# Gated cross-attention with a mixture of experts: eight normalised tiles made by ScalarE instead of VectorE

## What is computed

```
x: (2, 1024, 256)   ctx: (2, 64, 256)   16 heads of 64   8 experts, 2 used per batch
xn  = layernorm(x)
q   = xn @ Wq ; k = ctx @ Wk / 8 ; v = ctx @ Wv          (per head)
x1  = x + tanh(g_xattn) * (softmax(q k^T) v @ Wo + bo)
y   = layernorm(x1)
pick 2 experts per batch from mean_over_tokens(y) @ gate_w ; shares from a softmax over the two
out = x1 + tanh(g_ffn) * sum_e share_e * (gelu(y @ w1[e] + b1[e]) @ w2[e] + b2[e])
```

## Time and profile before

| | |
|---|---|
| median of three runs | 321.4 us (321.29 to 321.45) |
| span of the profiled execution | 319.0 us (its total is not given; the runs lie 2.4 us above the span) |
| VectorE busy | 236.4 us, 563 instructions |
| ScalarE busy | 164.6 us, 577 instructions |
| GpSimd busy | 84.4 us, 158 instructions |
| chain that ended last | PE 73%, POOL 10%, issue 7%, DVE 6%, ACT 2% |
| mean granted TensorE clock | 0.999 of full speed |

### The profile page before, as it was taken

The page is one execution under the profiler, slowest core; times in us unless marked ns, Lnnn a source line. Parts: engine busy times, 40 slices in busy tenths (PEclk is TensorE's granted clock), DMA queues, the critical chain, the costliest instruction groups (busy, mean ns, idle before and its releaser), DMA issues.

```text
span 319.0 us, 5709 instructions
## 1 busy us (share of the span) xinstructions
PE 313.3 (98%) x1861; PEld 269.8 (85%) x1861; DVE 236.4 (74%) x563; ACT 164.6 (52%) x577; POOL 84.4 (26%) x158
## 2 busy tenths in 40 slices
PE   8999999999999999999999999999999999999996
PEld 7978997879988999888788888888887899888896
DVE  1989999889989998999998475566766554442643
ACT  2658575686766768766466254443542442321320
POOL 1416547585476655526500000000000000000000
PEclk9999999999999999999999999999999999999999
DMA  7997200300000009500016340000020000000012
GB/s 275 385 322 10 33 3 1 134 1 3 0 0 3 0 4 346 179 3 0 2 8 256 95 171 0 0 0 0 33 100 2 2 0 0 2 0 0 4 64 67
DMA packets 21918, 19.99 MB, mean 63 GB/s; under 512 B 11708, under 2 KB 17540, under 8 KB 21508
## 3 DMA queue, kind: packets, MB, share of 16 engines
q1 hardware_dynamic: 21616, 19.14, 20.0%
q10 hardware_dynamic: 276, 0.52, 0.4%
HBM read 17.56 MB, written 2.11 MB: 62 GB/s over the span
## 4 chain that ended last, share of the span: by engine, by line
PE 73%; POOL 10%; issue 7%; DVE 6%; ACT 2%; DMA 1%; POOLq 0%; DVEq 0%
PE ps L1154 22%; PE ps L1155 22%; PE ps L1156 22%; POOL sx L504 4%; PE ps L1174 2%; POOL xs L524 2%; PE ps L1239 2%; POOL xs L522 2%; ACT sx L636 1%; DMA wk_sb<-in_L_xattn_Wk_dram 1%; DVE mx L904 1%; PE ps L1196 1%; DVE pT_lo L863 1%; PE ps L1327 1%; DVE sm L874 1%
## 5 line engine op out<-in xcount | busy, mean ns | idle before, releaser
L723 ACT ACTIVATE gel<-ps,b1sel 128x512 f32<-128x512 f32 x64 | 43.9, 690 | 95.5 <-PE ps L1156 95.5
L1113 DVE CAST h_hi<-gel 128x512 fp32r<-128x512 f32 x64 | 28.4, 444 | 58.8 <-ACT gel L723 58.5
L636 ACT ACTIVATE sx<-ps,mx 128x64 f32<-128x64 f32 x128 | 38.3, 325 | 26.4 <-DVE mx L904 26.3
L1154 PE MATMUL ps<-yT_hi,w_hi 128*128 128x512 f32 (+1 forms) x128 | 50.5, 395 | 0.0
L1155 PE MATMUL ps<-yT_lo,w_hi 128*128 128x512 f32 (+1 forms) x128 | 50.0, 390 | 0.0
L1156 PE MATMUL ps<-yT_hi,w_lo 128*128 128x512 f32 (+1 forms) x128 | 49.9, 390 | 0.0
L1115 DVE TENSOR_TENSOR h_lo<-gel,h_hi 128x512 fp32r<-128x512 f32 x64 | 44.9, 701 | 2.2
L504 POOL TENSOR_TENSOR sx<-sx,rs 128x512 f32<-128x512 f32 x32 | 33.5, 1066 | 41.5 <-DVE rs L879 40.8
L1154 PE MATMUL ps<-h_hi,w_hi 128*128 128x512 f32 x96 | 38.4, 400 | 0.0
L1156 PE MATMUL ps<-h_hi,w_lo 128*128 128x512 f32 x96 | 37.5, 390 | 0.0
L1155 PE MATMUL ps<-h_lo,w_hi 128*128 128x512 f32 x96 | 37.4, 390 | 0.0
(11 more groups left out here) (149 smaller groups left out, 670.0 us busy)
## 6 DMA issues: line engine op xcount, KB each, us to landing
stage_w<-in_L_ffn_w_dram SPq DMA_DIRECT2D x7, 1024.0 KB, 7.4
out_dram<-xt SPq DMA_DIRECT2D x6, 256.0 KB, 2.3
wqT<-in_L_xattn_Wq_dram SPq DMA_DIRECT2D x2, 512.0 KB, 6.9
wv_sb<-in_L_xattn_Wv_dram SPq DMA_DIRECT2D x2, 512.0 KB, 8.5
wo_sb<-in_L_xattn_Wo_dram SPq DMA_DIRECT2D x1, 1024.0 KB, 13.4
xt<-in_x_dram SPq DMA_DIRECT2D x1, 1024.0 KB, 10.4
xs<-in_xT_dram SPq DMA_DIRECT2D x1, 1024.0 KB, 11.2
spread<-x_stat SPq DMA_DIRECT2D x1, 1024.0 KB, 4.6
```

The costliest lines, as they stand in the source:

```text
L636: last = nc.scalar.activation(sx[:, par, c0:c0 + M], ps[:, 2 * par + 1, c0 - BANK:c0 - BANK + M], ACT.Exp, bias=mx[:, par, h:h + 1], accum ...
L723: nc.scalar.activation(gel[:, f % 4, :], ps[:, h_bank, :], ACT.Gelu, bias=b1sel[:, b, slot, f:f + 1]).then_inc(gelu_done, 1)
L1113: nc.vector.tensor_copy(h_hi[:, f % 4, :], gel[:, f % 4, :]).then_inc(hhi_ready, 1)
L1154: mm(acc, hi_w, hi_x, start=start, stop=False)
```

## The change

The VectorE function `y_tile` and its calls are gone. ScalarE has a `y_tile` in its place, called in its step s after `y_high` and before the late `vw` groups and `heads(s)`. It computes scale * x + bias, with scale = rstd2 and bias = shift2 = -mean2 * rstd2. The new small tensor `shift2` is made by GpSimd with two instructions behind the Newton steps, for the parts of the first batch, ahead of the post of `y_rstd`. The waits on `y_rstd` and on the buffer (`yT_done`) are the same and are now ScalarE's.

```
+    shift2 = place("shift2", [P, TB])
...
             def y_rstds(i):
 
                 newton(*Y_PARTS[i], rstd2, ve_y, len(X_PARTS) + i + 1)
+                if Y_PARTS[i][0] < TB:
+                    tiles = slice(*Y_PARTS[i])
+                    link(nc.gpsimd.tensor_tensor(shift2[:, tiles], mean2[:, tiles], rstd2[:, tiles], ALU.mult))
+                    link(nc.gpsimd.tensor_scalar(shift2[:, tiles], shift2[:, tiles], -1.0, None, ALU.mult))
                 pool.sem_inc(y_rstd, 1)
...
+            def y_tile(t):
+
+                act.wait_ge(y_rstd, t // 4 + 1)
+                wait_pos(act, yT_done, t - 1)
+                nc.scalar.activation(yb[:, t % 2, :], xt[:, t, :], ACT.Identity, scale=rstd2[:, t:t + 1],
+                                     bias=shift2[:, t:t + 1]).then_inc(y_ready, 1)
...
                 for y in (Y_WITH_X.get(s), Y_AFTER.get(s)):
                     if y is not None:
                         y_high(y, 7, D, y + 1)
+                for y in (Y_WITH_X.get(s + 1), Y_AFTER.get(s + 1)):
+                    if y is not None:
+                        y_tile(y)
                 if s == NT - 1:
                     w1_high(0)
...
                 if s == 14:
                     y_guess((s - 6) // 4)
-                for y in (Y_WITH_X.get(s + 1), Y_AFTER.get(s + 1)):
-                    if y is not None:
-                        y_tile(y)
...
-            def y_tile(t):
-
-                dve.wait_ge(y_rstd, t // 4 + 1)
-                wait_pos(dve, yT_done, t - 1)
-                nc.vector.tensor_scalar(yb[:, t % 2, :], xt[:, t, :], mean2[:, t:t + 1], rstd2[:, t:t + 1],
-                                        ALU.subtract, ALU.mult).then_inc(y_ready, 1)
```

## The result

The changed kernel takes 324.07 us (median, 323.86 to 324.32), the kernel before 321.35 us (321.04 to 321.45). The ratio is 1.0078, 95% interval 1.0056 to 1.0100: 2.5 us slower (1.8 to 3.2). The prediction was 324.2. The span of the profiled execution went from 319.0 to 321.9 us. Busy time moved as intended, VectorE from 236.4 down to 231.0 us and ScalarE from 164.6 up to 168.0.

What follows compares the result with a forecast made beforehand. TensorE, 98% busy, was taken as the bound, with the ScalarE-VectorE loop of 6.95 us close behind. 2.30 - 0.65 - 0.48 + 0.59 + 1.00 = 2.76 us on the median of 321.4 gave 324.2 us, range 322.3 to 325.3.

Steps and rivals of the forecast that it cites:

- The three places: Where lateness arises: ScalarE's hold in step 7, GpSimd's added time at tile 10, two y tiles ahead of heads 12.
- GpSimd's p = 0.59: Time of GpSimd's two added instructions behind the Newton steps in steps 7 and 11: 0.59 us, bounds 0.40 and 0.8.
- ScalarE's x = 0.50: ScalarE's time for one 128x256 y tile with per-partition scale and bias: 0.50 us, bounds 0.31 and 1.0.
- The hold of step 7, 2.30: In step 7 ScalarE's y tile 0 waits for the first y_rstd, making heads of tile 7 2.30 us late.
- the slack of step 10, 0.48: In step 10 VectorE's pT_lo started 0.48 us later than it could, so that much lateness is absorbed.
- slack of 0.65: VectorE's pT_lo of tile 6 started 0.65 us later than it could, so 2.30 us of lateness leaves 1.65.
- Step 11 and 12: Tile 10's product 1.76 us late; two y tiles ahead of heads of tile 12 add 1.00, making 2.76.
- (a): Rival, 12%: buffers absorb step 7's hold; only 0.59 at 98.86 and part of step 12 reach TensorE: 0.6 to 1.3, 322.4 us.
- (b): Rival, 12%: none of the 0.65 + 0.48 slack absorbs anything and a y tile takes 0.66: 4.4, 325.8 us.
- (c): Rival, 6%: y tiles arrive early, TensorE's waits of 0.31 + 0.26 go, decided in step 7: 320.8 us.
- (d): Rival, 6%: gains and losses cancel over the kernel, within 0.6 us, 321.4.
- 0.08 + 2p + 3x: The whole forecast slowdown in GpSimd's added time p and ScalarE's time per y tile x: 2.76 us.

Runs made afterwards that it cites:

- pool_only: The kernel before with only GpSimd's two small instructions per Newton part added, result unread, VectorE still making all y tiles; 321.70 us, ratio 1.0011.
- one_pool_op: The changed kernel with one GpSimd instruction instead of two, VectorE's statistics halving the mean sum with -0.5 for the first batch; 323.26 us, ratio 1.0054.
- tiles67_dve: The changed kernel with y tiles 6 and 7 made by VectorE again, ScalarE making tiles 0 to 5; 323.31 us, ratio 1.0064.
- best_c: The changed kernel with one GpSimd instruction, three y buffers, and y tiles 6 and 7 ahead of the wait for tile 5's transpose; 322.54 us, ratio 1.0044.
- best_split: best_c with GpSimd's Newton steps begun one step earlier, 8 of 13 instructions in its idle wait; 320.69 us, ratio 0.9977.
- before_split: The kernel before, y tiles on VectorE, with only GpSimd's Newton steps begun one step earlier; 320.93 us, ratio 0.9991.
- after_split: The changed kernel with GpSimd's Newton steps begun one step earlier, 8 of 13 instructions in its idle wait; 321.31 us, ratio 1.0000.
- act_only: The changed kernel without GpSimd's two instructions, ScalarE taking mean2 as bias, so y is shifted wrongly; 322.30 us, ratio 1.0035.

## Why the prediction was right

The three places and the way they add up were right. The sum of 2.76 us met 2.7 in the trace (2.62 at TensorE's last instruction) and 2.5 (1.8 to 3.2) timed. That it fits to a tenth is partly luck, since two of its terms were each wrong by about 0.25 us, in opposite directions. The 2.4 us that the prediction puts on top of the span compare one execution's span with the median of others; by their own spans nearly all executions here lie 2.0 us above it. The forecast is the median of before plus the sum, so this does not enter it. Step by step:

*What is removed.* Right that the eight VectorE instructions are worth almost nothing where they stood: they lay under heads, and VectorE's wait for pT_hi grew from 1.4 to 8.3 us. TensorE's two waits for y tiles went, as said, but a new wait of 0.34 us for tile 6's product, at 71.45, stands in the place of the first, so nothing was won by it: y tile 0 is 0.11 late.

*GpSimd's p = 0.59.* GpSimd's rows of step 7, with the last Newton instruction (477), the second new one (485) and the product behind it (509):

```profile
68.38 0.20 POOL L477 TENSOR_TENSOR rstd<-nu_p,rstd 128x4 f32<-128x4 f32 x1
...
68.94 0.23 POOL L485 TENSOR_SCALAR shift<-shift 128x4 f32<-128x4 f32 x1
69.35 2.04 POOL L509 TENSOR_TENSOR sx<-sx,rs 128x512 f32<-128x512 f32 x2 [0.18 <-POOL shift L485]
```

From the end of the Newton steps at 68.58 to the end of the new instructions at 69.17 it is 0.59. pool_only and one_pool_op showed that it counts at tile 10 and, with tiles on ScalarE, a second time through the hold. One reading was inexact without consequence: the prediction adds 2.10 to 96.76, and the row has 2.04, so the product ended at 98.80, 0.06 before TensorE started.

*ScalarE's x = 0.50.* Measured 0.51 in step 7 (69.25 to 69.76) and 0.49 in step 12 (106.52 to 107.50 for two). The latency was 0.587 to 0.687 us by the y tile's row in the trace, median 0.60, where I had 0.66. The Trainium skill, "ScalarE: Activation LUTs", section What ACT_TABLE_LOAD costs, gives 186 ns plus 0.833 ns per element and about 93 ns for each per-partition operand, with 93 ns of overlap. The estimate from these figures for 256 elements and two such operands is 0.585 us, and 0.49 us to the next instruction. The trace agrees: 0.587 us at the least, 0.49 and 0.51 to the next instruction. The rule of the same page that I weighed in the prediction, VectorE for adds and multiplies, is given there for bf16 and was no guide to the price in float32.

*The hold of step 7, 2.30, and the slack of step 10, 0.48.* These two terms were wrong and cancelled by luck. Heads of tile 7 were 2.07 late, not 2.30. I had counted 1.35 us from the vw groups to heads, but in the kernel before the row maxima ended only at 68.52, and heads started at 68.55 right behind them. In the changed kernel the maxima are long there, and it is 1.14 (69.76 to 70.90). pT_lo of tile 6 was 1.42 late, so the slack of 0.65 held, and steps 8 and 9 added nothing, as forecast (heads 1.43 and 1.41 late). Then step 10 took up 0.23, not 0.48: pT_lo of tile 8 was 1.19 late. The rows of VectorE and GpSimd in the changed kernel show where the rest went:

```profile
85.83 0.43 DVE L967 BATCH_NORM_STATS2 stats<-xt 128x6 f32<-128x256 f32 x1
86.29 0.70 DVE L777 TENSOR_TENSOR dm<-stats 128x4 f32<-128x4 f32 x1
86.91 0.15 DVE L778 TENSOR_TENSOR mean<-stats 128x4 f32<-128x4 f32 x1
```

```profile
86.08 0.89 POOL L529 TENSOR_TENSOR xs<-xs,spread 128x256 f32<-128x256 f32 x1
```

A 4-column instruction with two SBUF inputs took 0.70 us instead of 0.17, and it ended with GpSimd's, at 86.99 against 86.97. In the kernel before it started at 85.34, after GpSimd's had ended at 85.30. So 1.19 us entered step 11, where 1.17 was forecast.

*Step 11 and 12.* 1.17 + 0.59 = 1.76 at tile 10, measured 1.78. TensorE's wait before it was 1.01 + 0.35 = 1.36 us, not 1.7, because TensorE came to it later than I had thought (y tile 3 was 0.62 late). Heads of tile 12 2.76 late, measured 2.77. The transpose of y tile 7 2.76, measured 2.70, waiting for yT_lo as said (0.67 us, not 1.0: TensorE was 1.89 late at y tile 6 already). tiles67_dve and best_c confirm that the last 1.0 us comes from these two tiles and their place: without them there it falls to 1.9 and, with the smaller p, 1.3.

*Rivals.* (a), that the hold is absorbed, and (b), that no slack exists, fall with the column of heads 7 against y4: 2.07 + 0.59 arrives as 1.78. (c) needed `y_rstd` before about 67.9, and the Newton steps ended later. best_split meets that condition and ends 0.64 us early, near the 0.57 of (c), but this does not show (c)'s mechanism: before_split ends 0.35 early with every y tile still on VectorE. (d), that both cancel, is what after_split does, and the change does not.

What stays open: that GpSimd's access is what stretched VectorE's small instruction in step 10 was not tested by a run of its own. The kept traces support it. The same instruction takes 0.70 to 0.72 us in all five kernels where GpSimd's instruction was under way when it started (after, act_only, one_pool_op, tiles67_dve, best_c), each time ending 0.02 to 0.03 us behind it, and 0.16 to 0.17 in the eight others, where none was. How best_split's edits share its gain beyond what is said above was not divided up either.

## What to carry to other kernels

Before work is moved from a busy engine to an idle one, read what its in-order queue has behind the new place and when the input is there: here the semaphore that VectorE never waited for, because it came to it late, held ScalarE idle for 2.8 us with heads behind it, and heads came 2.07 us late. One instruction may count several times: p and x came into the sum as 0.08 + 2p + 3x. Where two loops are nearly equal, a saving on one is soon stopped by the other: TensorE's own pace is 6.70 us per step where it never waits (best_split, y tiles 0 to 4), that of ScalarE and VectorE 6.95, and of the 1.32 us that TensorE was ahead 0.52 were left at y tile 7. So produce the late input earlier, in a neighbour's idle wait, before shifting the consumer, and measure the shift against a kernel that has the early input too.

## What the runs showed of the hardware that was not expected

A VectorE instruction on 128x4 with both inputs in SBUF took 0.70 us where it started behind a GpSimd instruction on 128x256 in SBUF, and 0.15 to 0.17 where none was under way or the one that was had 0.14 us or less left. The kernel before has such meetings too, in an earlier step:

```profile
47.10 0.72 DVE L763 TENSOR_TENSOR mean<-stats 128x8 f32<-128x8 f32 x1
...
47.94 0.71 DVE L765 TENSOR_SCALAR mean<-mean 128x8 f32<-128x8 f32 x1
```

```profile
47.06 0.74 POOL L522 TENSOR_TENSOR xs<-xs,spread 128x256 f32<-128x256 f32 x1
47.88 0.75 POOL L524 TENSOR_TENSOR xs<-xs,spread 128x256 f32<-128x256 f32 x1
```

VectorE's instructions end at 47.82 and 48.65, GpSimd's at 47.80 and 48.63. The second of VectorE's has only one input. So in these cases the small instruction lasted as long as the rest of the other one. The Trainium skill, "SBUF — State Buffer", section Who interferes with whom, says that a VectorE instruction with two SBUF inputs contends with a GpSimd one that reads SBUF, over a port pair that one of them holds alone; the ends at 86.99 and 86.97 agree. In the prediction I had asked only what the large y tile does to GpSimd. It was the small instruction that moved, in the one step where VectorE could have caught up.
